# Another order of the instructions of a state-space group on four engines of a three-stage decoder layer

## The chip, the cores and the metric

The kernel runs on one core of a Trainium2 chip, as one program in one launch. The metric is the device time of that launch in microseconds (us). TensorE (PE in the profile; PEld is its weight load), VectorE (DVE), ScalarE (ACT) and GpSimd (POOL) each execute their own stream of instructions in order; SyncE (SP) issues most of the transfers. The engines are tied to each other only by semaphores: an instruction that waits holds up everything that stands behind it on its engine.

## The reference

The input x has 64 sequences of 128 tokens of 128 features. The layer is three blocks, each followed by a residual sum and a layer norm:

```
xz = x @ W_in;  xb, z = halves of xz (256 channels each)
xb = silu(causal conv of 4 taps over xb, + conv_b)
dt_low, B, C = split(xb @ W_x)           # 64, 16, 16
dt = softplus(dt_low @ W_dt + b_dt)
h[t] = h[t-1] * exp(A * dt[t]) + (x[t] * dt[t]) * B[t]   # 256 channels x 16 states
y[t] = sum over the 16 states of h[t] * C[t];  y = y + xb * D
x = layernorm(x + (y * silu(z)) @ W_out)                 # state-space block
x = layernorm(x + slots(x, context))                     # 3 rounds of slot attention and GRU
x = layernorm(x + expert(x))                             # one of 8 experts per token
```

Only the first block is touched by the change.

## The kernel before

**Stages.** `mamba_stage` (the state-space block) and `slot_stage` share one block of engine programs, `expert_stage` follows. All float32. The state-space stage treats 16 groups of 4 sequences (512 tokens), one after the other, features on the 128 partitions and tokens along the free dimension. The 256 channels are two halves c = 0, 1 and there are 16 states n, so a group has 32 units (n, c).

**One unit.** ACT computes the decays exp(A dt) of a unit (`decay`); the input (dt x) B comes in one of three ways; DVE runs the recurrence as one scan over 512 tokens (`scan`, L734); POOL multiplies both halves of the state by C (`product`, L440, written here p0 to p15) into one of four `hc` buffers; PE adds that into `ps_y` by eight transposing matmuls (`add_y`, L914).

**Three ways for the input.** States 1, 5 and 9 are fed by POOL (`feed`, L425: dtx times a row of B that a transfer has spread over the partitions). States 0, 2, 4, 8, 10, 12, 13 and 15 are fed by DVE (`feed`, L717, which reads B from the one PSUM bank `ps_b`, filled by PE in `spread_b`, L923). States 3, 6, 7, 11 and 14 are "side" states: ACT scales a transposed dtx by B (`scaled`, four instructions, L574), PE transposes it into a `ps_op` bank (`side_input`, L931), and the decays go into `da_side` instead (L564).

**Buffers that set the order.** `inp`, `state` and `hc` have four slots, used by n mod 4. A POOL feed of state n waits until scan (n-4, 1) is done, a scan (n, 0) until product n-4 is done, a product until add_y n-4 is done. The three `ps_op` banks go round over the units, so a direct decay (or the side input) of a unit waits until the scan three units earlier is done. `da_side` and `inpT` have two slots. The two `ps_misc` banks serve all the rest: the projections of the next group, the tail of the group before, and the units P, K, V0, V1, V2 that prepare the context for the slot stage.

**Across groups.** While group g is scanned, the same engines prepare group g+1 (transposed x, convolution, `silu`, `x_dbl`, B transposed, dt, dtx) and finish group g-1: DVE gates y with z after the last add_y of g-1 (`gated`, L705, in the middle of the scans of state 2), PE turns and projects it, ACT centres and squares it, and DVE multiplies by 1/std at the end of group g (`normed`, L710, whose two inputs `cent` and `lnv` both lie in SBUF). Then DVE feeds state 0 of group g+1. POOL computes dt and dtx of g+1 between products 11 and 12.

**What fixes the order.** No planner runs: in each engine's program a function `group` lists the calls by hand, and `over_groups` unrolls it 16 times (`first` and `last` leave parts out). In the text f5 is a feed of state 5, s(5,1) the scan of unit (5,1), and a prime marks the next group. SP has its own list, with waits on those engines before its transfers.

Of the kernel before, what the change touches and what calls it, by code (L numbers as in the profile page):

```python
# [12 lines left out]
P = 128  # L13
# [111 lines left out]
def mamba_stage(nc, t, sb, psum, sem, blk, tail, slot_in, x1T, ident, made, NG, NS, C, R):  # L125
# [272 lines left out]
    def _(pool):  # L398
# [43 lines left out]
        def group(g, par, first, last):  # L442
            product(g, par, first, 0)
            product(g, par, first, 1)
            product(g, par, first, 2)
            feed(g, par, 5)
            product(g, par, first, 3)
            product(g, par, first, 4)
            feed(g, par, 9)
            product(g, par, first, 5)  # L450
            product(g, par, first, 6)
            product(g, par, first, 7)
# [11 lines left out]
            product(g, par, first, 14)  # L464
            if not last:
                feed(g + 1, 1 - par, 1)
            product(g, par, first, 15)
# [3 lines left out]
    def _(act):  # L471
# [128 lines left out]
        def group(g, par, first, last):  # L600
            if not first:
                read_unit(g - 1, "V2")
            if not last:
                prepare(g + 1, 1 - par, "xT")
            decay(g, par, 1, 0)
            scaled(g, par, 3)
# [23 lines left out]
            if not first:  # L630
                turned(g - 1, 0)
# [3 lines left out]
            decay(g, par, 9, 0)  # L635
            if not last:
                prepare(g + 1, 1 - par, "BT")
            scaled(g, par, 11)
            if not last:
                prepare(g + 1, 1 - par, "relu0")  # L640
            decay(g, par, 9, 1)
            if not first:
                turned(g - 1, 1)
            if not last:
                prepare(g + 1, 1 - par, "abs0")
            decay(g, par, 10, 0)
            decay(g, par, 10, 1)
            decay(g, par, 11, 0)
            if not last:
                prepare(g + 1, 1 - par, "relu1")  # L650
                prepare(g + 1, 1 - par, "abs1")
            decay(g, par, 11, 1)
            if not last:
                prepare(g + 1, 1 - par, "exp")
            decay(g, par, 12, 0)
            decay(g, par, 12, 1)
            if not first:
                centred(g - 1)
            if not last:
                prepare(g + 1, 1 - par, "ln")  # L660
            read_unit(g, "P")
            decay(g, par, 14, 0)
            scaled(g, par, 14)
            decay(g, par, 13, 0)
            read_unit(g, "K")
            decay(g, par, 13, 1)
            decay(g, par, 14, 1)
            if not first:
                log_variance(g - 1)
                root(g - 1)  # L670
# [14 lines left out]
    def _(dve):  # L685
# [52 lines left out]
        def group(g, par, first, last):  # L738
            scan(g, par, 0, 0)
            scan(g, par, 0, 1)  # L740
            feed(g, par, 2)
            scan(g, par, 1, 0)
            scan(g, par, 1, 1)
            scan(g, par, 2, 0)
# [3 lines left out]
            scan(g, par, 3, 0)  # L748
            scan(g, par, 3, 1)
            feed(g, par, 4)  # L750
# [4 lines left out]
            feed(g, par, 8)  # L755
# [32 lines left out]
    def _(pe):  # L788
# [166 lines left out]
        def group(g, par, first, last):  # L955
            if not first:
                add_y(g - 1, 1 - par, 14)
# [3 lines left out]
            if not first:  # L961
                add_y(g - 1, 1 - par, 15)
# [1330 lines left out]
```

## Time and profile before

| | us |
|---|---|
| median of 3 runs | 1535.23 (1533.06 to 1535.28) |
| the profiled execution's own time | 1535.57 |
| its span in the profile | 1533.7 |
| busy: PE / DVE / ACT / POOL | 1375.4 / 1215.4 / 1105.4 / 1222.6 |
| mean granted clock of PE | 0.964 |

The span is what the profile covers from the first to the last instruction; the execution's own time holds 1.87 us more. Busy times are sums over the three stages. The state-space stage lasts from the start to about 850 us, the slot stage from there to some 1330 us, the expert stage to the end. In a timeline a row is one run of like instructions: start, length, engine, line, operation, output and inputs, and in brackets how long the engine sat idle before it and who released it. Neighbouring instructions of an engine overlap by some hundredths of a microsecond in such rows, so what an instruction costs on its engine is the distance between two starts.

### The profile page before, as it was taken

How to read it: one execution, taken by the hardware profiler on the slowest of the kernel's cores; microseconds unless marked ns; L12 is line 12 of the kernel's file. 1: busy time of each engine (PE TensorE's matmuls, PEld its weight loads, DVE VectorE, ACT ScalarE, POOL GpSimd, SP SyncE). 2: the span in 40 equal slices, each digit the busy share in tenths (PEclk: the TensorE clock that was granted, in tenths of full speed). 3: DMA queues.
4: the chain of work that ended last, by engine and by line, in shares of the span. 5: the costliest groups of instructions: out<-in, count | busy, mean ns of one | idle time of the engine just before them, and what ended most of it. 6: DMA issues, size and time to landing. Idle time of an engine off the chain costs nothing. (4 is left out here: it accounts for less than half of the span.)

```text
span 1533.7 us, 27686 instructions
## 1 busy us (share of the span) xinstructions
PE 1375.4 (90%) x8898; PEld 1075.9 (70%) x8898; DVE 1215.4 (79%) x2143; ACT 1105.4 (72%) x2296; POOL 1222.6 (80%) x845
## 2 busy tenths in 40 slices
PE   5999999999999999999988899999999999559993
PEld 2676766666766676677666688878888877449993
DVE  1899999999999999999999477777777777734552
ACT  3888988889888988898887666666666665115552
POOL 1899999999999999999998544577777776625665
PEclk8999999999999999999999999999999999669997
DMA  4334433434344434443341642431436000057770
GB/s 139 103 99 140 124 123 104 130 124 132 95 131 123 136 97 125 128 131 110 117 127 60 205 144 103 150 122 57 154 130 254 9 8 15 21 152 193 207 215 28
DMA packets 114560, 182.75 MB, mean 119 GB/s; under 512 B 12210, under 2 KB 75637, under 8 KB 114432
## 3 DMA queue, kind: packets, MB, share of 16 engines
q1 hardware_dynamic: 109888, 172.68, 36.5%
q0 software_dynamic: 4544, 8.47, 1.6%
q8 instruction: 67, 1.10, 0.3%
q14 instruction: 61, 0.50, 0.1%
HBM read 126.37 MB, written 55.66 MB: 119 GB/s over the span
## 5 line engine op out<-in xcount | busy, mean ns | idle before, releaser
L440 POOL TENSOR_TENSOR hc<-state,c_rows 128x1024 f32<-128x1024 f32 x256 | 599.4, 2367 | 26.4 <-DVE state L734 26.3
L734 DVE TENSOR_TENSOR_SCAN state<-ps_op,inp 128x512 f32<-128x512 f32 x352 | 406.5, 1203 | 7.8 <-issue 3.3
L914 PE MATMUL ps_y<-ident,hc 128*128 128x128 f32 x2048 | 255.5, 274 | 22.0 <-POOL hc L440 21.7
L914 PEld LDWEIGHTS ps_y<-ident,hc 128*128 128x128 f32 x2048 | 228.4, 141 | 63.9 <-POOL hc L440 47.3
L567 ACT ACTIVATE ps_op<-dt,a_neg 128x512 f32<-128x512 f32 x352 | 238.5, 690 | 40.5 <-DVE state L734 36.6
L734 DVE TENSOR_TENSOR_SCAN state<-da_side,ps_op 128x512 f32<-128x512 f32 x160 | 183.9, 1197 | 16.4 <-PE ps_op L931 16.4
L717 DVE TENSOR_TENSOR inp<-dtx,ps_b 128x1024 f32<-128x1024 f32 x128 | 153.5, 1199 | 44.1 <-POOL dtx L413 24.0
L1325 POOL TENSOR_TENSOR rs<-ms,m_half 128x4 f32<-128x4 f32 x48 | 68.0, 1416 | 117.2 <-DVE ms L1584 117.0
L1493 ACT ACTIVATE ex<-sc,nmx,ctx_r 77x128 f32<-77x128 f32 x192 | 92.4, 482 | 91.1 <-DVE nmx L1597 91.1
L574 ACT ACTIVATE inpT<-dtxT,b_tok 128x256 f32<-128x256 f32 x320 | 135.8, 499 | 0.0
L425 POOL TENSOR_TENSOR inp<-dtx,b_rows 128x1024 f32<-128x1024 f32 x48 | 120.1, 2502 | 0.0
L2103 POOL DMA_INDIRECT out_x<-orow,target x78 | 77.0, 987 | 43.4 <-ACT orow L2124 22.3
L564 ACT ACTIVATE da_side<-dt,a_neg 128x512 f32<-128x512 f32 x160 | 109.7, 715 | 0.0
L931 PEld LDWEIGHTS ps_op<-ident,inpT 128*128 128x128 f32 x640 | 73.2, 142 | 47.7 <-issue 30.5
L931 PE MATMUL ps_op<-ident,inpT 128*128 128x128 f32 x640 | 96.2, 278 | 9.3 <-DVE state L734 6.5
L923 PE MATMUL ps_b<-ident,b_tok 128*128 128x128 f32 x512 | 80.6, 281 | 25.2 <-DVE inp L717 25.2
L2134 ACT ACTIVATE act_h<-ps_h 128x512 f32<-128x512 f32 x78 | 46.5, 597 | 69.2 <-PE ps_h L2244 59.6
L923 PEld LDWEIGHTS ps_b<-ident,b_tok 128*128 128x128 f32 x512 | 58.4, 139 | 52.7 <-DVE inp L717 32.8
L1423 POOL DMA_INDIRECT sorted_x<-row,dest x60 | 62.1, 1036 | 26.4 <-issue 14.5
L2253 PEld LDWEIGHTS ps_yy<-w,act_h 128*128 128x128 f32 x624 | 75.6, 192 | 2.0
L2253 PE MATMUL ps_yy<-w,act_h 128*128 128x128 f32 x624 | 75.8, 275 | 0.0
L2244 PE MATMUL ps_h<-xcol,w 128*128 128x256 f32 x312 | 75.5, 386 | 0.0
(251 smaller groups left out, 3141.6 us busy)
## 6 DMA issues: line engine op xcount, KB each, us to landing
c_rows<-bc_rows SPq DMA_DIRECT2D x128, 512.0 KB, 3.8
sorted_x<-pad_rows SPq DMA_DIRECT2D x8, 4160.0 KB
w<-in_L_ffn_W SPq DMA_DIRECT2D x78, 256.0 KB
b_rows<-bc_rows SPq DMA_DIRECT2D x48, 256.0 KB, 4.9
vw<-vw_rows SPq DMA_DIRECT2D x16, 462.0 KB
vw_rows<-vw_out SPq DMA_DIRECT2D x16, 384.0 KB
xrow<-sorted_x SPq DMA_DIRECT2D x39, 130.0 KB
x_tok<-in_x SPq DMA_DIRECT2D x16, 256.0 KB, 4.5
```

The lines of the kernel that those rows point to most:

```text
L425: pool.tensor_tensor(inp[:, n % RING], dtx[:, par], over_c(b_rows[:, s]), ALU.mult).then_inc(pool_fed, 1)
L440: pool.tensor_tensor(hc[:, n % RING], state[:, n % RING], over_c(c_rows[:, slot, n % 2]), ALU.mult).then_inc(hc_ready, 1)
L564: act.activation(da_side[:, at % 2, c], dt[:, par, c], ACT.Exp, scale=a_neg[:, c, n:n + 1]).then_inc(side_da, 1)
L567: act.activation(op_bank(g, n, c)[:], dt[:, par, c], ACT.Exp, scale=a_neg[:, c, n:n + 1]).then_inc(da_ready, 1)
L574: ins = act.activation(inpT[:, at % 2, b], dtxT[:, b].rearrange("p c d -> p (c d)"), ACT.Copy, scale=b_tok[:, par, b, n:n + 1])
L717: dve.tensor_tensor(inp[:, n % RING], dtx[:, par], over_c(ps_b[:]), ALU.mult).then_inc(dve_fed, 1)
L734: dve.tensor_tensor_scan(state[:, n % RING, c], decays, inputs, 0.0, ALU.mult, ALU.add).then_inc(state_ready, 1)
L914: ins = pe.matmul(ps_y[:, b, c], hc[:, n % RING, c, b * P:(b + 1) * P], ident[:], start=False, stop=n == NS - 1, is_transpose=True, skip_g ...
L923: ins = pe.transpose(ps_b[:, b * P:(b + 1) * P], b_tok[:, par, b, n:n + 1].broadcast_to([P, P]), ident[:])
L931: ins = pe.transpose(op_bank(g, n, c)[:, b * P:(b + 1) * P], inpT[:, at % 2, b, c * P:(c + 1) * P], ident[:])
L1493: act.activation(ex[p][0:M, b * P:(b + 1) * P], sc[p][:, b * P:(b + 1) * P], ACT.Exp, bias=nmx[p][:, b:b + 1], scale=ctx_r[:, g % RING, b: ...
L2253: ins = pe.matmul(ps_yy[par][:, s * P:(s + 1) * P], act_h[:, par, c, s * P:(s + 1) * P], w2[:, buf, c], start=c == 0, stop=c == FC - 1)
```

## The change

Nothing is added or removed. In `group` on POOL, ACT, DVE and PE the same calls stand in another order; buffers, semaphores, the transfers of SP and the other stages are as before. On POOL, the feed of state 5 moves ahead of product 0, that of state 9 behind product 6, and that of state 1 of the next group ahead of product 14. On DVE most feeds stand one or two scans later and `normed` stays at the end. On ACT the decays of state 3 and 11 come earlier, `scaled` of 11 stands between the two loads of activation tables, and `root` comes later. On PE the side inputs and spreads are placed anew among the add_y.

```diff
--- before.py
+++ after.py
@@ pool: group @@
 def group(g, par, first, last):
+    feed(g, par, 5)
     product(g, par, first, 0)
     product(g, par, first, 1)
     product(g, par, first, 2)
-    feed(g, par, 5)
     product(g, par, first, 3)
     product(g, par, first, 4)
-    feed(g, par, 9)
     product(g, par, first, 5)
     product(g, par, first, 6)
+    feed(g, par, 9)
     product(g, par, first, 7)
     product(g, par, first, 8)
     product(g, par, first, 9)
...
     if not last:
         prepare(g + 1, 1 - par, "first")
     product(g, par, first, 13)
+    if not last:
+        feed(g + 1, 1 - par, 1)
     product(g, par, first, 14)
-    if not last:
-        feed(g + 1, 1 - par, 1)
     product(g, par, first, 15)
@@ scalar: group @@
 def group(g, par, first, last):
+    decay(g, par, 3, 0)
+    if not last:
+        prepare(g + 1, 1 - par, "xT")
+    decay(g, par, 1, 0)
+    decay(g, par, 1, 1)
     if not first:
         read_unit(g - 1, "V2")
-    if not last:
-        prepare(g + 1, 1 - par, "xT")
-    decay(g, par, 1, 0)
     scaled(g, par, 3)
-    decay(g, par, 1, 1)
     decay(g, par, 2, 0)
-    decay(g, par, 3, 0)
-    decay(g, par, 2, 1)
     decay(g, par, 3, 1)
     decay(g, par, 6, 0)
+    decay(g, par, 2, 1)
+    scaled(g, par, 6)
+    scaled(g, par, 7)
     decay(g, par, 6, 1)
-    scaled(g, par, 6)
     decay(g, par, 4, 0)
-    scaled(g, par, 7)
+    decay(g, par, 4, 1)
     decay(g, par, 7, 0)
+    decay(g, par, 5, 0)
     decay(g, par, 7, 1)
-    decay(g, par, 4, 1)
-    decay(g, par, 5, 0)
     decay(g, par, 5, 1)
     act.preload_act_table_set("silu_and_others")
     if not last:
         prepare(g + 1, 1 - par, "xb0")
         prepare(g + 1, 1 - par, "xb1")
+    scaled(g, par, 11)
     gates(g, 0)
     gates(g, 1)
     act.preload_act_table_set("natural_log_exp_and_others")
     decay(g, par, 8, 0)
+    decay(g, par, 8, 1)
+    if not last:
+        prepare(g + 1, 1 - par, "dbl")
     if not first:
         turned(g - 1, 0)
-    decay(g, par, 8, 1)
-    if not last:
-        prepare(g + 1, 1 - par, "dbl")
+    decay(g, par, 11, 0)
+    if not last:
+        prepare(g + 1, 1 - par, "BT")
     decay(g, par, 9, 0)
-    if not last:
-        prepare(g + 1, 1 - par, "BT")
-    scaled(g, par, 11)
+    decay(g, par, 9, 1)
     if not last:
         prepare(g + 1, 1 - par, "relu0")
-    decay(g, par, 9, 1)
-    if not first:
-        turned(g - 1, 1)
-    if not last:
         prepare(g + 1, 1 - par, "abs0")
     decay(g, par, 10, 0)
     decay(g, par, 10, 1)
...
+    decay(g, par, 11, 1)
+    scaled(g, par, 14)
...
-    decay(g, par, 11, 1)
+    if not first:
+        turned(g - 1, 1)
...
         prepare(g + 1, 1 - par, "exp")
     decay(g, par, 12, 0)
+    read_unit(g, "P")
+    if not last:
+        prepare(g + 1, 1 - par, "ln")
     decay(g, par, 12, 1)
+    decay(g, par, 13, 0)
     if not first:
...
+    decay(g, par, 13, 1)
     decay(g, par, 14, 0)
-    scaled(g, par, 14)
-    decay(g, par, 13, 0)
     read_unit(g, "K")
-    decay(g, par, 13, 1)
-    decay(g, par, 14, 1)
     if not first:
         log_variance(g - 1)
+    decay(g, par, 14, 1)
+    decay(g, par, 15, 0)
+    read_unit(g, "V0")
+    decay(g, par, 15, 1)
+    if not last:
+        prepare(g + 1, 1 - par, "t0")
+    if not first:
         root(g - 1)
-    read_unit(g, "V0")
-    decay(g, par, 15, 0)
-    decay(g, par, 15, 1)
+    if not last:
+        decay(g + 1, 1 - par, 0, 0)
     read_unit(g, "V1")
     if not last:
-        prepare(g + 1, 1 - par, "t0")
-        decay(g + 1, 1 - par, 0, 0)
         prepare(g + 1, 1 - par, "t1")
         decay(g + 1, 1 - par, 0, 1)
@@ vector: group @@
 def group(g, par, first, last):
     scan(g, par, 0, 0)
     scan(g, par, 0, 1)
-    feed(g, par, 2)
     scan(g, par, 1, 0)
     scan(g, par, 1, 1)
+    feed(g, par, 2)
     scan(g, par, 2, 0)
     if not first:
         gated(g - 1)
     scan(g, par, 2, 1)
     scan(g, par, 3, 0)
+    feed(g, par, 4)
     scan(g, par, 3, 1)
-    feed(g, par, 4)
     scan(g, par, 4, 0)
...
     scan(g, par, 5, 1)
-    feed(g, par, 8)
...
-    feed(g, par, 10)
+    feed(g, par, 8)
     scan(g, par, 8, 0)
     scan(g, par, 8, 1)
+    feed(g, par, 10)
...
     scan(g, par, 11, 0)
+    feed(g, par, 12)
     scan(g, par, 11, 1)
-    feed(g, par, 12)
     feed(g, par, 13)
     scan(g, par, 12, 0)
     scan(g, par, 12, 1)
+    scan(g, par, 13, 0)
     feed(g, par, 15)
-    scan(g, par, 13, 0)
     scan(g, par, 13, 1)
     scan(g, par, 14, 0)
     scan(g, par, 14, 1)
@@ tensor: group @@
 def group(g, par, first, last):
+    spread_b(g, par, 2)
+    if not last:
+        fill_misc(g + 1, 1 - par, "xb1")
     if not first:
         add_y(g - 1, 1 - par, 14)
-    spread_b(g, par, 2)
-    if not last:
-        fill_misc(g + 1, 1 - par, "xb1")
+    if not last:
+        fill_misc(g + 1, 1 - par, "xb0")
     if not first:
         add_y(g - 1, 1 - par, 15)
-    if not last:
-        fill_misc(g + 1, 1 - par, "xb0")
+    side_input(g, 3, 0)
+    side_input(g, 3, 1)
     spread_b(g, par, 4)
-    side_input(g, 3, 0)
     if not last:
         fill_misc(g + 1, 1 - par, "xb0+")
-    side_input(g, 3, 1)
+        fill_misc(g + 1, 1 - par, "xb1+")
     start_y(g, par)
-    if not last:
-        fill_misc(g + 1, 1 - par, "xb1+")
     add_y(g, par, 0)
     add_y(g, par, 1)
-    add_y(g, par, 2)
     spread_b(g, par, 8)
     side_input(g, 6, 0)
+    add_y(g, par, 2)
     side_input(g, 6, 1)
     fill_z(g, 0, last)
+    side_input(g, 7, 0)
     fill_z(g, 1, last)
-    side_input(g, 7, 0)
-    spread_b(g, par, 10)
     side_input(g, 7, 1)
...
     add_y(g, par, 3)
+    spread_b(g, par, 10)
     if not last:
         fill_misc(g + 1, 1 - par, "BT")
-    add_y(g, par, 4)
     if not first:
         turn_y(g - 1, 1)
+    if not last:
+        fill_misc(g + 1, 1 - par, "dt0")
+    add_y(g, par, 4)
+    if not last:
+        fill_misc(g + 1, 1 - par, "dt1")
+    side_input(g, 11, 0)
     add_y(g, par, 5)
+    spread_b(g, par, 12)
     add_y(g, par, 6)
+    side_input(g, 11, 1)
     add_y(g, par, 7)
-    if not last:
-        fill_misc(g + 1, 1 - par, "dt1")
     add_y(g, par, 8)
-    side_input(g, 11, 0)
-    side_input(g, 11, 1)
+    fill_unit(g, "P", last)
+    spread_b(g, par, 13)
     if not first:
         project(g - 1)
-    fill_unit(g, "P", last)
+    spread_b(g, par, 15)
     add_y(g, par, 9)
-    spread_b(g, par, 13)
-    spread_b(g, par, 15)
+    add_y(g, par, 10)
     fill_unit(g, "K", last)
     if not first:
...
     side_input(g, 14, 0)
-    add_y(g, par, 10)
+    side_input(g, 14, 1)
     fill_unit(g, "V0", last)
-    side_input(g, 14, 1)
+    if not last:
+        fill_misc(g + 1, 1 - par, "t0")
     add_y(g, par, 11)
     if not last:
         spread_b(g + 1, 1 - par, 0)
     fill_unit(g, "V1", last)
     if not last:
-        fill_misc(g + 1, 1 - par, "t0")
+        fill_misc(g + 1, 1 - par, "t1")
     add_y(g, par, 12)
-    fill_unit(g, "V2", last)
-    if not last:
-        fill_misc(g + 1, 1 - par, "t1")
+    add_y(g, par, 13)
     if g + 2 < NG:
         fill_misc(g + 2, par, "xT")
-    add_y(g, par, 13)
+    fill_unit(g, "V2", last)
```

## Rows read from the trace of the kernel before

**Rows 1.** The page: busy time, share of the span and instructions, by engine.
```profile
PE 1375.4 (90%) x8898; PEld 1075.9 (70%) x8898; DVE 1215.4 (79%) x2143; ACT 1105.4 (72%) x2296; POOL 1222.6 (80%) x845
```
**Rows 2.** Busy time in one period of group 7 (stretch, length, engines, PE clock, DMA).
```profile
391.81:442.40 50.59, 46.94 (x294) 34.16 (x293) 48.08 (x43) 45.09 (x81) 49.35 (x24) 1.00 0.41 121
```
**Rows 3.** Timeline of POOL over one period (start, length, what, idle before).
```profile
391.81 2.83 POOL L425 TENSOR_TENSOR inp<-dtx,b_rows 128x1024 f32<-128x1024 f32 x1
394.61 4.67 POOL L440 TENSOR_TENSOR hc<-state,c_rows 128x1024 f32<-128x1024 f32 x2
399.45 2.38 POOL L440 TENSOR_TENSOR hc<-state,c_rows 128x1024 f32<-128x1024 f32 x1 [0.18 <-DVE state L734]
402.81 2.36 POOL L440 TENSOR_TENSOR hc<-state,c_rows 128x1024 f32<-128x1024 f32 x1 [0.98 <-DVE state L734]
405.12 2.38 POOL L425 TENSOR_TENSOR inp<-dtx,b_rows 128x1024 f32<-128x1024 f32 x1
...
414.41 16.29 POOL L440 TENSOR_TENSOR hc<-state,c_rows 128x1024 f32<-128x1024 f32 x7
430.66 2.35 POOL L409 TENSOR_TENSOR dt<-relu,softp 128x1024 f32<-128x1024 f32 x1
...
435.41 2.38 POOL L440 TENSOR_TENSOR hc<-state,c_rows 128x1024 f32<-128x1024 f32 x1
...
442.40 2.84 POOL L425 TENSOR_TENSOR inp<-dtx,b_rows 128x1024 f32<-128x1024 f32 x1
```
**Rows 4.** Timeline of DVE over the same period.
```profile
390.53 1.88 DVE L710 TENSOR_TENSOR x1T<-cent,sq 128x512 f32<-128x512 f32 x1
392.34 1.21 DVE L717 TENSOR_TENSOR inp<-dtx,ps_b 128x1024 f32<-128x1024 f32 x1
393.68 2.34 DVE L734 TENSOR_TENSOR_SCAN state<-ps_op,inp 128x512 f32<-128x512 f32 x2
...
411.79 4.54 DVE L734 TENSOR_TENSOR_SCAN state<-da_side,ps_op 128x512 f32<-128x512 f32 x4
...
425.45 2.33 DVE L734 TENSOR_TENSOR_SCAN state<-da_side,ps_op 128x512 f32<-128x512 f32 x2 [0.95 <-PE ps_op L931]
...
429.95 1.22 DVE L717 TENSOR_TENSOR inp<-dtx,ps_b 128x1024 f32<-128x1024 f32 x1 [1.05 <-PE ps_b L923]
```
**Rows 5.** Timeline of POOL in the first and in the last group.
```profile
40.25 2.35 POOL L440 TENSOR_TENSOR hc<-state,c_rows 128x1024 f32<-128x1024 f32 x1 [1.14 <-DVE state L734]
46.43 4.69 POOL L440 TENSOR_TENSOR hc<-state,c_rows 128x1024 f32<-128x1024 f32 x2 [3.83 <-DVE state L734]
...
807.79 2.36 POOL L440 TENSOR_TENSOR hc<-state,c_rows 128x1024 f32<-128x1024 f32 x1 [1.00 <-DVE state L734]
...
838.47 2.38 POOL L440 TENSOR_TENSOR hc<-state,c_rows 128x1024 f32<-128x1024 f32 x1 [2.81 <-DVE state L734]
841.83 7.42 POOL L440 TENSOR_TENSOR hc<-state,c_rows 128x1024 f32<-128x1024 f32 x3 [0.98 <-DVE state L734]
```
**Rows 6.** Timeline of DVE at the end of the last group.
```profile
846.12 0.93 DVE L710 TENSOR_TENSOR x1T<-cent,sq 128x512 f32<-128x512 f32 x1
```
**Rows 7.** Timeline of ACT: first group, then `scaled` and the table load of group 7.
```profile
42.20 0.70 ACT L567 ACTIVATE ps_op<-dt,a_neg 128x512 f32<-128x512 f32 x1
...
393.07 1.70 ACT L574 ACTIVATE inpT<-dtxT,b_tok 128x256 f32<-128x256 f32 x4
...
408.17 1.28 ACT L622 ACT_TABLE_LOAD   x1
...
412.85 1.28 ACT L628 ACT_TABLE_LOAD   x1
414.15 0.69 ACT L567 ACTIVATE ps_op<-dt,a_neg 128x512 f32<-128x512 f32 x1
```
**Rows 8.** Timeline of PE in group 7: add_y of product 15, and half a convolution.
```profile
397.01 1.09 PE L914 MATMUL ps_y<-ident,hc 128*128 128x128 f32 x8 [1.05 <-POOL hc L440]
397.94 1.88 PE L806 MATMUL ps_misc<-x1T,w_conv 128*128 128x512 f32 x4
```

More of the change, by code:

```diff
@@ L463, in group @@
             product(g, par, first, 13)
-            product(g, par, first, 14)
             if not last:
                 feed(g + 1, 1 - par, 1)
+            product(g, par, first, 14)
             product(g, par, first, 15)
@@ L605, in group @@
             decay(g, par, 1, 0)
+            decay(g, par, 1, 1)
+            if not first:
+                read_unit(g - 1, "V2")
             scaled(g, par, 3)
-            decay(g, par, 1, 1)
             decay(g, par, 2, 0)
-            decay(g, par, 3, 0)
-            decay(g, par, 2, 1)
             decay(g, par, 3, 1)
             decay(g, par, 6, 0)
+            decay(g, par, 2, 1)
+            scaled(g, par, 6)
+            scaled(g, par, 7)
             decay(g, par, 6, 1)
-            scaled(g, par, 6)
             decay(g, par, 4, 0)
-            scaled(g, par, 7)
+            decay(g, par, 4, 1)
             decay(g, par, 7, 0)
+            decay(g, par, 5, 0)
             decay(g, par, 7, 1)
-            decay(g, par, 4, 1)
-            decay(g, par, 5, 0)
             decay(g, par, 5, 1)
@@ L629, in group @@
             decay(g, par, 8, 0)
-            if not first:
-                turned(g - 1, 0)
             decay(g, par, 8, 1)
@@ L634, in group @@
                 prepare(g + 1, 1 - par, "dbl")
-            decay(g, par, 9, 0)
+            if not first:
+                turned(g - 1, 0)
+            decay(g, par, 11, 0)
             if not last:
                 prepare(g + 1, 1 - par, "BT")
-            scaled(g, par, 11)
+            decay(g, par, 9, 0)
+            decay(g, par, 9, 1)
             if not last:
                 prepare(g + 1, 1 - par, "relu0")
-            decay(g, par, 9, 1)
+                prepare(g + 1, 1 - par, "abs0")
+            decay(g, par, 10, 0)
+            decay(g, par, 10, 1)
+            if not last:
+                prepare(g + 1, 1 - par, "relu1")
+            decay(g, par, 11, 1)
+            scaled(g, par, 14)
+            if not last:
+                prepare(g + 1, 1 - par, "abs1")
             if not first:
@@ L955, in group @@
         def group(g, par, first, last):
-            if not first:
-                add_y(g - 1, 1 - par, 14)
             spread_b(g, par, 2)
@@ L961, in group @@
             if not first:
-                add_y(g - 1, 1 - par, 15)
+                add_y(g - 1, 1 - par, 14)
             if not last:
                 fill_misc(g + 1, 1 - par, "xb0")
+            if not first:
+                add_y(g - 1, 1 - par, 15)
+            side_input(g, 3, 0)
+            side_input(g, 3, 1)
             spread_b(g, par, 4)
-            side_input(g, 3, 0)
             if not last:
                 fill_misc(g + 1, 1 - par, "xb0+")
-            side_input(g, 3, 1)
+                fill_misc(g + 1, 1 - par, "xb1+")
             start_y(g, par)
-            if not last:
-                fill_misc(g + 1, 1 - par, "xb1+")
             add_y(g, par, 0)
             add_y(g, par, 1)
-            add_y(g, par, 2)
             spread_b(g, par, 8)
             side_input(g, 6, 0)
+            add_y(g, par, 2)
             side_input(g, 6, 1)
             fill_z(g, 0, last)
+            side_input(g, 7, 0)
             fill_z(g, 1, last)
-            side_input(g, 7, 0)
-            spread_b(g, par, 10)
             side_input(g, 7, 1)
@@ L988, in group @@
             add_y(g, par, 3)
+            spread_b(g, par, 10)
             if not last:
                 fill_misc(g + 1, 1 - par, "BT")
+            if not first:
+                turn_y(g - 1, 1)
+            if not last:
+                fill_misc(g + 1, 1 - par, "dt0")
             add_y(g, par, 4)
             if not last:
-                fill_misc(g + 1, 1 - par, "dt0")
+                fill_misc(g + 1, 1 - par, "dt1")
+            side_input(g, 11, 0)
+            add_y(g, par, 5)
             spread_b(g, par, 12)
-            if not first:
-                turn_y(g - 1, 1)
-            add_y(g, par, 5)
             add_y(g, par, 6)
+            side_input(g, 11, 1)
             add_y(g, par, 7)
-            if not last:
-                fill_misc(g + 1, 1 - par, "dt1")
             add_y(g, par, 8)
-            side_input(g, 11, 0)
-            side_input(g, 11, 1)
+            fill_unit(g, "P", last)
+            spread_b(g, par, 13)
             if not first:
                 project(g - 1)
-            fill_unit(g, "P", last)
+            spread_b(g, par, 15)
             add_y(g, par, 9)
-            spread_b(g, par, 13)
-            spread_b(g, par, 15)
+            add_y(g, par, 10)
             fill_unit(g, "K", last)
```

10 lines of the change are left out of this document (1 added, 9 removed).

## The prediction

> **What bounds the kernel now.** I read the busy line first [rows 1]: PE is busiest by name, but its rows overlap, and over the whole span nothing is full. The share has to be read in the stage that the change touches. The stretch table for one period of group 7 [rows 2] has POOL busy 49.35 of 50.59 us, DVE 48.08, PE 46.94 and ACT 45.09. The reader should see two engines within 5% of the period, and POOL the fuller one.
>
> The timeline of POOL says the same from start to start [rows 3]. The feed of state 1 starts at 391.81 and again at 442.40, so the period is 50.59 us. POOL is idle in it twice: 0.18 us ahead of p1 (399.45) and 0.98 us ahead of p2 (402.81), both released by a scan. The rest, 50.59 - 1.16 = 49.43 us, is work; I use 49.4. Its price list: a product 2.32 us (seven take 16.25 us, 414.41 to 430.66), f5 as a feed without a neighbour 2.3, dt and dtx together 4.75 (430.66 to 435.41), the feed of state 1 2.79 (391.81 to 394.61, two hundredths off by rounding).
>
> The price of that last feed, and the two idle times, have one cause, which the timeline of DVE shows [rows 4]. `normed` starts at 390.53 and takes 1.88 us. In the last group the same instruction takes 0.93 us [rows 6], so its length isn't work. In both places it ends about 0.6 us after POOL's next instruction could begin: 390.53 + 1.88 = 392.41 = 391.81 + 0.60 in group 7. In the last group the three products from 841.83 cost 7.42 us [rows 5] where three at 2.32 are 7.0. So `normed` waits for the POOL instruction in flight to end, then runs 0.6 us, and POOL's next one loses 0.47 us (2.79 against 2.32). The Trainium skill says so of the pair of SBUF ports that the two engines share (SBUF — State Buffer, Who interferes with whom): a DVE instruction with two SBUF inputs and a GpSimd one that reads SBUF exclude each other, for a whole instruction. By that rule, and the rows agree, the time of `normed` moves in steps of one POOL instruction.
>
> Now the cycle that makes 50.59 closes. From the end of p14 (391.81) DVE needs normed 0.53, the feed of state 0 1.34 (392.34 to 393.68), then s(0,0) to s(2,1) with one feed and `gated` between, eight steps of 1.12 us, to release p2 at 402.81, 11.0 us later. From p2 POOL runs without a gap to the end of the next p14. DVE's own waits for PE, 0.95 and 1.05 us [rows 4], lie ahead of the port wait and are swallowed by it.
>
> **The change, part by part.** Nothing is added to any list, so every term is a wait.
>
> POOL, feed of state 5 moved ahead of p0: it needs scan (1,1) only. Where POOL came to p2 after two products and needed s(2,1), it now comes to f5 straight behind p15 and needs s(1,1), and reaches p2 one instruction later; the close meeting moves from s(2,1) to s(1,1). With t = 0 at the start of f5 and POOL never idle: p0 2.3, p1 4.7, p2 7.0, p3 9.3, p5 13.9, f9 18.6, p8 23.2, p11 30.2, dt 32.5, dtx 34.9, p12 37.2, p13 39.6, feed 1' 41.9, p14 44.7, p15 47.0, next f5 49.4. If `normed` is queued before p13 ends at 41.9, it goes there; then the feed of state 0' is at 42.4, s(0,0)' at 43.8, and s(1,1)' ends at 48.35, or t = -1.0 of the next group. f5 finds it ready with 1.0 us to spare. No row shows POOL waiting for s(1,1) at f5, so I bound that wait by 0 and by the 0.98 us of p2 before; I take 0, and keep the upper end for the rival called leaks. Below nothing it can't go, since POOL's own work stays.
>
> DVE from there, with steps of 1.12 us (three steps and 1.19 are the 4.54 of four scans [rows 4]) and 1.34 where a scan reads the feed just ahead of it: s(2,1) ends at 3.8 (p2 wants it at 7.0), s(3,1) 7.2 (p3 9.3), s(5,1) 11.7 (p5 13.9), s(8,1) 19.7 (p8 23.2), s(11,1) 29.0 (p11 30.2, the narrowest), s(15,1) 40.4. In it are three waits that I find by laying the new lists of ACT and PE beside each other: `gated` 0.15 us, since half a convolution (steps of 1.7 us, from the 1.88 of [rows 8]) now stands ahead of add_y 15 (1.09, same rows); s(9,0) 0.4 us for f9, which starts later and ends at 20.9; the feed of state 13 0.3 us for its spread. They replace the two of 0.95 and 1.05. So `normed` is queued at 40.4, 1.5 us before the 41.9 at which it must be there. That 1.5 us is the cover of every wait not seen.
>
> ACT: 45.09 us of work in 49.4 [rows 2]. Its dangerous stretch is table load, two silu, `scaled` of 11, two gates, table load, decay (8,0). `scaled` (1.6 us of pitch, 1.70 in [rows 7]) is new in it. I get the first table load at 9.1, `scaled` at 11.95 (it waits for side input (6,1)), decay (8,0) done at 16.7, and s(8,0) wants it at 17.4: hidden by 0.7 us, and costing DVE one for one beyond that. A load costs 1.30 us from start to the next start (412.85 to 414.15 [rows 7]). The Trainium skill (ScalarE: Activation LUTs, What ACT_TABLE_LOAD costs) gives 1283 ns and 1380 ns of drain behind it, about 2.66 us in all. The trace doesn't show the drain here; by the page's figure decay (8,0) would be 2.8 us later, DVE would miss 41.9, and the rival of one step below would hold. I go by the rows.
>
> PE: 46.94 us in 49.4, 2.5 us of slack [rows 2]. The closest meetings I find are side input (14,0), ready 0.2 us before s(14,0), and side (7,1), 0.4 us before s(7,1). If each such meeting came 0.5 us late instead, the 1.5 us would just be spent. The transfers of C rows follow products p1, p3, ... as before, and the first user is six products behind; moved feeds release the B rows more than 15 us before use. `root` is done at 39.2, before `normed`. I cost all these at nothing; without that cover the price is that of a POOL step.
>
> **Sum.** (a) First group: p0 ran at 40.25 in the shade of the start-up, p1 from 46.43, p2 from 46.43 + 2.31 = 48.74 [rows 5]. Now f5 stands first and waits for s(1,1). Decay (1,0) started at 42.20 after the copy of x [rows 7] and still does, so the scan goes at 42.9, s(1,1) ends at 45.2, f5 starts at 45.3 and p2 at 52.3: +3.5 us. (b) From p2 of group 0 to p2 of group 15: before 807.79 - 48.74 = 759.05 us; now 14 periods of 49.4 and one without `normed` of 48.9, 740.5 us: -18.5. (c) Last group, p2 to the end of p15: p15 ended at 841.83 + 7.42 = 849.25, so before 849.25 - 807.79 = 41.46, with 2.81 and 0.98 of waits [rows 5]. Now POOL is held by DVE from p12 on; s(15,1) ends at 40.4, p15 runs from 40.5 to 43.3 with the 0.47 of the port, and 43.3 - 7.0 = 36.3: -5.1. Together -20.1 us, of which 2.3 in (a) and (c) is f5 changing sides of p2. The stages behind shift as they are. That assumes a POOL without a gap of even a tenth in 15 periods; I give back 0.07 us in each, 1 us. The profiled execution has 1535.57 us (its span of 1533.7 and 1.87 around it), so 1535.57 - 19.1 = 1516.5; the median before is 0.34 lower, which gives 1516.
>
> **Rivals.** *One step late.* If DVE's waits in a group reach some 1.5 us more than I found, `normed` misses the end of p13 and goes at the end of the feed of state 1', at 44.2. Then s(1,1)' ends at 44.2 + 0.53 + 1.34 + 4.56 + a hand-off of 0.1 = 50.75, and that is the period. (b) becomes 14 x 50.75 + 48.9 = 759.4, (a) + (b) + (c) = 3.5 + 0.4 - 5.1 = -1.2 us: 1534, no change. For it: the old waits of 2.00 us, kept in full and added to the 0.85 that I count, would do it. Against: both belonged to places in the PE list that have moved (spread 13 stood behind three adds and `project`, side input 11 behind add_y 8).
>
> *Two steps late,* the slower side. The same port: should DVE be held 3.4 us or more (the point is `normed` queued after 44.2 in the slower cycle), it goes at the end of p14, 2.32 us later again. The period is 53.1, (b) grows by 14 x 2.32 = 32.5: 1566. The place would be the ACT block around the table loads. For it: `scaled` 11 in the block, 0.7 us of cover. Against: the block would have to be 4 us longer than ACT's rows make it.
>
> *Leaks.* `normed` makes its step, but POOL meets late scans, at p11 or at f5 itself, for 0.3 to 1.0 us a group: 15 times that on 1515, so 1520 to 1530. For it: POOL has only 1.0 us in hand at f5 and 1.2 at p11. Against: DVE's schedule has 1.5 us of rest before the port in every group.
>
> *The order does nothing,* since another engine bounds the period. DVE has 48.08 us with 1.3 of port wait in it and the others less, so none reaches 50.6; I count it with one step late.
>
> **How the numbers follow.** Forecast 0.70 (1513 to 1519), leaks 0.14, one step late 0.10, two steps 0.06. A measurement can tell about 0.2%, 3 us, from no change. Faster by more is the forecast and the leaks: 0.84. Within 0.2%: 0.10. Slower: 0.06. The range 1512 to 1531 holds forecast and leaks with their bounds, 0.84 less the tails, and leaves the two late cases out. Below 1512 POOL would need less than its own work.
>
> **What would show it.** Right: a period of 49.4 from one feed of state 1 to the next; no idle of POOL within a group; the feed still 2.8; `normed` ending 0.6 us behind the end of p13, with a length between 1.5 and 2.5 us; DVE idle below 1.5 us a group, mainly at s(9,0) and the feed of state 13. Wrong: `normed` ending behind the feed of state 1' or p14; POOL waiting for scan (1,1) at f5 in every group (then the port cycle still rules); ACT's decay (8,0) released later than s(7,1); a PE clock below 1.00 in the middle groups, where two gaps on PE grow together.

## The result, and the profile after

The changed kernel takes 1517.93 us (median of 4 runs, 1516.06 to 1518.79) against 1535.26 of the kernel before, a ratio of 0.9891 with a 95% interval of 0.9879 to 0.9903: 17.3 us faster. The forecast was 1516. The profiled execution has a span of 1516.3 us.

The busy line of the page, and below it the stretch table for one period in mid-run (stretch, length, PE, PEld, DVE, ACT, POOL, PE clock, DMA share, GB/s), which answers to [rows 2]:

```profile
PE 1366.7 (90%) x8898; PEld 1080.4 (71%) x8898; DVE 1218.3 (80%) x2143; ACT 1099.4 (73%) x2296; POOL 1220.9 (81%) x845
```
```profile
386.03:435.41 49.38, 46.35 (x292) 34.39 (x292) 48.36 (x43) 44.78 (x81) 49.30 (x23) 1.00 0.40 125
```

The work is the same, and POOL fills 49.30 of 49.38 us. Its timeline over that period, beside [rows 3], has no bracket with an idle time left:

```profile
386.03 2.83 POOL L425 TENSOR_TENSOR inp<-dtx,b_rows 128x1024 f32<-128x1024 f32 x1
388.82 4.68 POOL L440 TENSOR_TENSOR hc<-state,c_rows 128x1024 f32<-128x1024 f32 x2
393.46 2.37 POOL L425 TENSOR_TENSOR inp<-dtx,b_rows 128x1024 f32<-128x1024 f32 x1
395.79 16.30 POOL L440 TENSOR_TENSOR hc<-state,c_rows 128x1024 f32<-128x1024 f32 x7
...
433.10 2.37 POOL L440 TENSOR_TENSOR hc<-state,c_rows 128x1024 f32<-128x1024 f32 x1
435.41 2.82 POOL L425 TENSOR_TENSOR inp<-dtx,b_rows 128x1024 f32<-128x1024 f32 x1
```

And DVE's, beside [rows 4]:

```profile
387.89 4.57 DVE L737 TENSOR_TENSOR_SCAN state<-ps_op,inp 128x512 f32<-128x512 f32 x4
...
414.55 4.57 DVE L737 TENSOR_TENSOR_SCAN state<-ps_op,inp 128x512 f32<-128x512 f32 x4 [0.30 <-POOL inp L425]
...
422.77 1.22 DVE L720 TENSOR_TENSOR inp<-dtx,ps_b 128x1024 f32<-128x1024 f32 x1 [0.31 <-PE ps_b L926]
...
433.97 2.04 DVE L713 TENSOR_TENSOR x1T<-cent,sq 128x512 f32<-128x512 f32 x1
435.94 1.21 DVE L720 TENSOR_TENSOR inp<-dtx,ps_b 128x1024 f32<-128x1024 f32 x1
```

`normed` (L713 now) is queued at 433.97 and p13 ends at 435.41, so it lies 1.44 us ahead of its step; it ends at 436.01, 0.60 us behind it. The four scans from 387.89 end at 392.46, and f5 starts at 393.46, 1.0 us later. The two waits of 0.95 and 1.05 us for PE are gone, and 0.30 and 0.31 stand in their place.

Two things in the trace weren't forecast. POOL waits for an add_y in group 5, in group 13 and in the last one. The first of them on POOL, then PE ahead of it, then PE's stretch table:

```profile
320.22 7.02 POOL L440 TENSOR_TENSOR hc<-state,c_rows 128x1024 f32<-128x1024 f32 x3 [0.80 <-PE ps_y L917]
```
```profile
315.35 1.12 PE L832 MATMUL ps_misc<-xdbl,w_dt 64*128 64x512 f32 x2 [0.33 <-ACT softp L506]
317.41 0.97 PE L934 MATMUL ps_op<-ident,inpT 128*128 128x128 f32 x4 [0.94 <-DVE state L737]
318.17 1.91 PE L917 MATMUL ps_y<-ident,hc 128*128 128x128 f32 x8
```
```profile
316.00:320.00 4.00, 3.06 (x15) 2.62 (x14) 4.00 (x5) 3.82 (x8) 3.43 (x2) 0.69 0.41 142
```

The eight matmuls of an add_y take 1.91 us here and 1.09 in [rows 8]. The granted clock averages 0.69 over these 4 us, so part of them ran at the lower of its two levels (1.2 GHz, not 2.4), behind idle times of 0.33 and 0.94 us on PE. The same two gaps stand in every group from 1 to 14; in twelve of these fourteen the clock stays at 1.00.

The time of the whole splits as follows. "Stage" is from POOL's first dt to the end of the last product. It leaves out the start-up, which ended anywhere between 31.7 and 34.8 us in the traces of this study, whatever the kernel.

| | median us | ratio to before, 95% | period us | stage us |
|---|---|---|---|---|
| before | 1535.26 | | 50.61 | 817.5 |
| changed | 1517.93 | 0.9891 [0.9879, 0.9903] | 49.38 | 800.6 |
| after_again | 1519.50 | 0.9903 [0.9887, 0.9920] | 49.38 | 800.2 |
| stretch2 | 1531.85 | 0.9978 [0.9963, 0.9993] | 49.38, then 50.85 | 810.0 |
| stretch4 | 1540.89 | 1.0040 [1.0028, 1.0053] | 50.85 | 823.0 |
| stretch6 | 1592.88 | 1.0380 [1.0363, 1.0397] | 54.61 | 875.1 |
| after_one_sbuf | 1513.85 | 0.9858 [0.9841, 0.9876] | 48.9 to 49.7 | 795.5 |
| before_one_sbuf | 1521.14 | 0.9913 [0.9896, 0.9930] | 49.57 | 802.7 |
| pool_only | 1572.51 | 1.0228 [1.0211, 1.0245] | 52.35 | 851.1 |
| all_but_pool | 1528.47 | 0.9943 [0.9926, 0.9960] | 49.74 | 806.3 |
| rest_feed1 | 1517.59 | 0.9885 [0.9869, 0.9902] | 49.38 | 799.2 |
| add5_first | 1517.83 | 0.9872 [0.9856, 0.9888] | 49.37 | 798.4 |
| rest_add5 | 1522.41 | 0.9911 [0.9891, 0.9931] | 49.72 | 802.5 |
| both | 1516.53 | 0.9875 [0.9857, 0.9892] | 49.38 | 796.2 |

The first two rows belong together. The others come from three chips: the `stretch` rows and after_one_sbuf from one, pool_only, all_but_pool, add5_first and rest_add5 from a second, the rest from a third. On these the kernel before took 1534.98, 1536.91 and 1535.23 us, so a row is read by its ratio to the kernel before on the same chip. Period and stage are those of one profiled execution each.

### The profile page after: what moved, and what is told of

It is laid out like the page before. It is cut to its first block and busy times, and to the rows that moved or that the text cites. A ratio compares the mean times of both kernels' runs of the same rounds, so it can differ in the third digit from the quotient of the medians.

```text
span 1516.3 us, 27686 instructions
## 1 busy us (share of the span) xinstructions
PE 1366.7 (90%) x8898; PEld 1080.4 (71%) x8898; DVE 1218.3 (80%) x2143; ACT 1099.4 (73%) x2296; POOL 1220.9 (81%) x845
## 5 line engine op out<-in xcount | busy, mean ns | idle before, releaser
L917 PE MATMUL ps_y<-ident,hc 128*128 128x128 f32 x2048 | 264.1, 276 | 23.2 <-POOL hc L440 23.1
L917 PEld LDWEIGHTS ps_y<-ident,hc 128*128 128x128 f32 x2048 | 232.6, 143 | 67.4 <-POOL hc L440 44.6
L934 PE MATMUL ps_op<-ident,inpT 128*128 128x128 f32 x640 | 93.0, 277 | 19.4 <-DVE state L737 19.3
L934 PEld LDWEIGHTS ps_op<-ident,inpT 128*128 128x128 f32 x640 | 75.8, 143 | 43.8 <-issue 40.4
```

The lines of the kernel that those rows point to most:

```text
L917: ins = pe.matmul(ps_y[:, b, c], hc[:, n % RING, c, b * P:(b + 1) * P], ident[:], start=False, stop=n == NS - 1, is_transpose=True, skip_g ...
L934: ins = pe.transpose(op_bank(g, n, c)[:, b * P:(b + 1) * P], inpT[:, at % 2, b, c * P:(c + 1) * P], ident[:])
```

## The experiments

In the expectations, "port theory" is the prediction's account: `normed` waits for the POOL instruction in flight, runs between it and the next, and so moves in steps of one POOL instruction.

### Does `normed` move in steps of a POOL instruction?

Three runs hold `normed` back, by two, four and six DVE reductions of 0.6 us each ahead of the last scan of a group. The edit with two, its declaration of `spare` left out:

```diff
         def scan(g, par, n, c):
...
+            if (n, c) == (15, 1):
+                for k in range(2):
+                    dve.tensor_reduce(spare[:, k:k + 1], decays, AX_X, ALU.add)
             dve.tensor_tensor_scan(state[:, n % RING, c], decays, inputs, 0.0, ALU.mult, ALU.add).then_inc(state_ready, 1)
```

> Changed kernel with four extra DVE reductions (2.4 us) ahead of the last scan of each group. Port theory: `normed` misses the end of p13 and goes behind the feed of state 1'; the period jumps to 50.75, 14 x 1.37 = 19 us plus 2.4 in the last group: 1537 to 1540, with POOL idle 1.3 us at f5. Rival (DVE's sum decides): 46.7 + 2.4 + 0.6 = 49.7 us, 14 x 0.3 + 2.4 = 7 us more: 1524 to 1526.

Measured: 1540.89 us, 0.9 above the range, and a period of 50.85, where the prediction's second cycle had 50.75. DVE and POOL of that run:

```profile
443.03 1.93 DVE L714 TENSOR_TENSOR x1T<-cent,sq 128x512 f32<-128x512 f32 x1
```
```profile
442.05 2.35 POOL L426 TENSOR_TENSOR inp<-dtx,b_rows 128x1024 f32<-128x1024 f32 x1
444.37 5.12 POOL L441 TENSOR_TENSOR hc<-state,c_rows 128x1024 f32<-128x1024 f32 x2
450.93 2.37 POOL L426 TENSOR_TENSOR inp<-dtx,b_rows 128x1024 f32<-128x1024 f32 x1 [1.44 <-DVE state L741]
```

`normed` is queued 1.0 us behind the start of the feed of state 1' (1.3 in most groups), so it waits to 444.37, ends 0.6 us later, and the loss of 0.46 us has moved from the feed (2.35 now) to the products behind it (5.12 for two). POOL idles 1.44 us at f5. The rival by sums is out: it had 1524 to 1526.

> Changed kernel with two extra DVE reductions (about 0.6 us each, results unused) ahead of the last scan of each group, so `normed` is queued 1.2 us later. Port theory: it is still queued before p13 ends (1.44 us of rest in the changed trace), so the period stays 49.4; only the last group, whose end hangs on DVE, is 1.2 us longer: 1518 to 1520. Rival (DVE's sum of work decides, no steps): DVE's 46.7 us of work and 0.6 of waits become 48.5, still under POOL's 49.4: the same 1518 to 1520.

Measured: 1531.85 us. Both theories missed. The period is 49.38 seven times (behind a first one of 48.9, without `normed`), once 50.1, and then 50.85 to the end. Where it turns:

```profile
515.72 7.03 POOL L441 TENSOR_TENSOR hc<-state,c_rows 128x1024 f32<-128x1024 f32 x3 [0.74 <-PE ps_y L921]
...
541.03 2.37 POOL L426 TENSOR_TENSOR inp<-dtx,b_rows 128x1024 f32<-128x1024 f32 x1 [1.43 <-DVE state L741]
```

With 1.2 us of reductions the queueing point lies 0.2 to 0.3 us ahead of the step. Ahead of the row at 515.72 PE's clock falls (0.72 on average from 512 to 518). POOL loses 0.74 us by it and DVE, which waits 1.16 us for a spread there, some 1.7, so `normed` is queued at 532.78, 0.6 us behind the end of p13, and the kernel never comes back: six groups in a row wait 1.43 to 1.45 us at f5. In the slower cycle f5 starts just behind its scan, not 1.0 us behind, so DVE starts each group that much later against POOL; this reason for its lasting is read from the trace, not tested. Two cycles last in the same kernel, and 1.2 us of extra work cost some 13 us by the ratios (0.9978 against 0.9891). The seven runs spread from 1526.74 to 1535.01 us, which would fit a slip in another group each time; only the one trace shows where.

> Changed kernel with six extra DVE reductions (3.6 us) ahead of the last scan of each group. Port theory: second step, `normed` behind p14, period 53.1, 14 x 3.7 = 52 us plus 3.6: 1571 to 1575. Rival (DVE's sum decides): 50.9 us, 14 x 1.5 + 3.6 = 25 us more: 1541 to 1544.

Measured: 1592.88 us, above either. Period 54.61, with 3.76 us of idle at f5, so the second step is taken; 1.5 us a group more than 53.1 remain, of which 1.16 us is p9 waiting for add_y 5, in nearly every group. PE's clock has a part in it, though not at the gap ahead of that add_y. With `normed` late, the feed of state 0' is late, and PE idles 3.99 us for it. The clock falls there in every period from 197 us on (0.53 on average from 416 to 423) and is back at 1.00 before 423, long before p9 waits:

```profile
417.26 1.12 PE L930 MATMUL ps_b<-ident,b_tok 128*128 128x128 f32 x4 [3.99 <-DVE inp L721]
418.17 3.61 PE L813 MATMUL ps_misc<-x1T,w_conv 128*128 128x512 f32 x4
```
```profile
425.73 1.23 DVE L709 TENSOR_TENSOR yz<-ps_y,sz 128x1024 f32<-128x1024 f32 x1 [1.35 <-PE ps_y L921]
```
```profile
449.05 7.02 POOL L441 TENSOR_TENSOR hc<-state,c_rows 128x1024 f32<-128x1024 f32 x3 [1.15 <-PE ps_y L921]
```

Half a convolution takes 3.61 us where [rows 8] has 1.88, the add_y behind it is late, `gated` waits 1.35 us, and from there DVE is late against POOL for side input (11,0), add_y 5 and p9. The last links are read from the rows; how much of the 1.16 us comes from the clock and how much from the later start of DVE isn't separated.

### Is it a conflict over the inputs in SBUF?

```diff
         def normed(g):
             dve.wait_ge(act_tail, atail("rstd", g))
-            dve.tensor_tensor(x_slot(g), cent[:], lnv[:], ALU.mult).then_inc(x1_ready, 1)
+            if g == NG - 1:
+                dve.tensor_tensor(x_slot(g), cent[:], lnv[:], ALU.mult).then_inc(x1_ready, 1)
+                return
+            if g + 2 < NG:
+                dve.wait_ge(b_spread, fed_count(DVE_FEEDS, g + 2, 0))
+            dve.tensor_tensor(x_slot(g), cent[:], ps_b[:], ALU.mult).then_inc(x1_ready, 1)
```

> Changed kernel in which `normed` takes its second input from the PSUM bank ps_b instead of the SBUF tile, in the groups 0 to 14 (so x1 is wrong, the normalisation is left out; same size, same count). Port theory: no wait for POOL and no loss on POOL's next feed: `normed` 0.6 us, the feed of state 1 2.32 instead of 2.79, period 48.9, 14 x 0.47 = 6.6 us less: 1510 to 1512. Rival (the 2.04 us of `normed` and the 2.8 us of the feed have other causes, as reading a tile just written): both lengths stay and so does the time, 1517 to 1519.

Measured: 1513.85 us. `normed` takes 0.66 us, all of the feeds of state 1 take 2.35 to 2.42, and the period is 48.9 to 49.0 in nine of its groups:

```profile
432.00 0.66 DVE L718 TENSOR_TENSOR x1T<-cent,ps_b 128x512 f32<-128x512 f32 x1
```
```profile
433.43 2.37 POOL L425 TENSOR_TENSOR inp<-dtx,b_rows 128x1024 f32<-128x1024 f32 x1
```

The instruction has another second operand, in another memory, and one semaphore wait more, for which DVE doesn't idle here; both the wait for POOL and POOL's loss of 0.47 us are gone. The trace of the changed kernel has the opposite case too: the `normed` of the last group, with both inputs in SBUF, runs while POOL is idle, and takes 0.68 us:

```profile
853.10 0.68 DVE L713 TENSOR_TENSOR x1T<-cent,sq 128x512 f32<-128x512 f32 x1
```

So two SBUF inputs alone don't make it long, nor does a tile just written; it is the two inputs meeting a POOL instruction, as the prediction had it. The time is 2 us above the forecast's upper end. In the groups 1 to 14 products waited five times for an add_y, 2.7 us in all, where the changed kernel has two such waits, 1.5 us together; that is 1.2 of it.

> The kernel before in which `normed` takes its second input from the PSUM bank ps_b instead of the SBUF tile, in the groups 0 to 14 (the normalisation is left out; same size, same count). Port theory: `normed` 0.6 us instead of 1.88 and the feed of state 1 2.35, so the chain from p14 to p2 is cut and POOL's 48.95 us or DVE's 49.3 decide: 14 x 1.3 to 1.6 us less, 1513 to 1518. Rival (DVE's waits for PE set POOL's idle time by themselves): they grow by what `normed` gives, and the time stays at 1530 to 1536.

Measured: 1521.14 us, 3.1 above the range: 14.1 us below the kernel before, where 17 to 22 were expected. The period of 49.57 keeps 0.6 us of idle at p2:

```profile
436.41 0.66 DVE L715 TENSOR_TENSOR x1T<-cent,ps_b 128x512 f32<-128x512 f32 x1
```
```profile
437.58 2.37 POOL L425 TENSOR_TENSOR inp<-dtx,b_rows 128x1024 f32<-128x1024 f32 x1
439.89 7.01 POOL L440 TENSOR_TENSOR hc<-state,c_rows 128x1024 f32<-128x1024 f32 x3
447.47 2.37 POOL L440 TENSOR_TENSOR hc<-state,c_rows 128x1024 f32<-128x1024 f32 x1 [0.56 <-DVE state L739]
```

One operand, with all old lists in place, gives most of what the reordering gave (14.1 us, against 15.7 for `after_again` on the same chip). So the port wait carried the old period. Of the 0.6 us that stays at p2, DVE's own waits (0.87 and 1.05 us for PE there, and about 0.5 ahead of s(10,0)) are the likely cause; no run takes them away with `normed` cut short.

### Which list does it?

`pool_only` is the kernel before with POOL's `group` of the changed one, `all_but_pool` the changed kernel with POOL's old one.

> The kernel before with only POOL's list in the new order. Port theory: f5 now waits for scan (1,1), which DVE's old list reaches one feed later; with `normed` at the end of p13 the period is 41.9 + 7.6 = 49.55, and with it one step later 51.9. DVE's queueing point falls 0.3 to 0.9 us before the end of p13, with all its old waits for PE, so it is one of two values: 1519 to 1522 where it is reached in every group, up to 1553 where it is missed, and one between where a slip in mid-run isn't made good. Rival (POOL's new order by itself removes POOL's idle time): 1516 to 1518.

Measured: 1572.51 us, 36 us slower than before; both theories missed. DVE, then POOL:

```profile
436.88 4.66 DVE L734 TENSOR_TENSOR_SCAN state<-ps_op,inp 128x512 f32<-128x512 f32 x4 [1.07 <-POOL inp L425]
443.11 2.33 DVE L734 TENSOR_TENSOR_SCAN state<-da_side,ps_op 128x512 f32<-128x512 f32 x2 [1.57 <-PE ps_op L931]
...
458.80 1.86 DVE L710 TENSOR_TENSOR x1T<-cent,sq 128x512 f32<-128x512 f32 x1
```
```profile
460.05 5.14 POOL L440 TENSOR_TENSOR hc<-state,c_rows 128x1024 f32<-128x1024 f32 x2
468.11 2.37 POOL L425 TENSOR_TENSOR inp<-dtx,b_rows 128x1024 f32<-128x1024 f32 x1 [2.92 <-DVE state L734]
```

f9 comes later in POOL's new list and now makes s(9,0) wait 1.07 us, which pushes the old wait for PE from 0.95 to 1.57; `normed` is queued behind the start of the feed of state 1' (it waits to 460.05), and f5, behind the old position of DVE's feed of state 2, waits 2.92 us. It is the late cycle, with the period 52.35 where I had 51.9. The forecast's upper value is still 20 us short. The stage is 33.6 us longer than before: 25.9 lie in the 14 periods, which run from 52.1 to 53.0, and 7.7 in the first and last group, for which the expectation had no price.

> The changed kernel with POOL's old list; DVE, ACT and PE in the new order. Port theory: DVE's waits for PE shrink from 2.0 to some 0.5 us, so `normed` is queued 1.9 us before the end of p13 and goes one POOL instruction earlier than before; p2 then finds its scan ready (0.8 us of rest) and the period is POOL's own 49.4. The first group keeps p0 ahead of f5, 1 to 2 us better than the changed kernel: 1515 to 1518. Rival (the moves on POOL are needed, since POOL's two idle times lie in front of p1 and p2): they stay, 1532 to 1536.

Measured: 1528.47 us, 8 us faster than before, neither of the two. The new lists of the three others do move `normed` one step earlier, but the period is 49.74:

```profile
443.46 2.34 DVE L737 TENSOR_TENSOR_SCAN state<-ps_op,inp 128x512 f32<-128x512 f32 x2 [1.08 <-POOL inp L425]
```
```profile
440.97 2.36 POOL L425 TENSOR_TENSOR inp<-dtx,b_rows 128x1024 f32<-128x1024 f32 x1
...
450.59 2.36 POOL L440 TENSOR_TENSOR hc<-state,c_rows 128x1024 f32<-128x1024 f32 x1 [0.30 <-DVE state L737]
```

With `normed` earlier, s(1,0)' arrives before its own feed, which stands behind p14 in POOL's old list, and waits 1.08 us; p2 pays 0.30. I had overlooked that feed. One move should mend it (the lists of the two runs against each other):

```diff
             product(g, par, first, 13)
+            if not last:
+                feed(g + 1, 1 - par, 1)
             product(g, par, first, 14)
-            if not last:
-                feed(g + 1, 1 - par, 1)
             product(g, par, first, 15)
```

> DVE, ACT and PE new, POOL's old list with one move, the feed of state 1' ahead of p14. Theory: the 1.08 us that scan (1,0) waits for this feed and the 0.30 us of p2 behind it go, the period is 49.4 instead of 49.74: 1520 to 1524. Rival (f5 ahead of p0 is what frees p2): still 0.3 us at p2, 1527 to 1529.

Measured: 1517.59 us, 2.4 below the range and 9 below the rival's, period 49.38, no wait of POOL in the groups 1 to 14. That equals the changed kernel (0.9885 against 0.9903 for `after_again` beside it, the intervals overlap). The moves of f5 and f9, which the prediction put first, aren't needed. Which of the three other lists, on DVE, ACT and PE, is needed was not tried.

### PE's clock, and the first group

```diff
-            side_input(g, 11, 0)
             add_y(g, par, 5)
+            side_input(g, 11, 0)
             spread_b(g, par, 12)
```

> The changed kernel with one pair on PE swapped: add_y 5 ahead of side input (11,0), which fills the gap of 0.95 us in which PE waits for a scan. Theory: in two groups and in the last one PE's granted clock fell behind that gap and a product waited 0.80, 0.68 and 1.20 us for add_y; these go: 1514 to 1517, and no POOL row with a wait for ps_y in the groups 1 to 14. Rival (the drops come by chance and anywhere): two or three such rows stay, 1517 to 1519.

Measured: 1517.83 us, above the forecast's range and inside the rival's, though on a chip on which the kernel before took 1.7 us more. But no product of any group waits for an add_y, and the stage is 798.4 us against 800.2 to 800.6. The gap is filled:

```profile
415.25 1.09 PE L917 MATMUL ps_y<-ident,hc 128*128 128x128 f32 x8
416.26 0.63 PE L934 MATMUL ps_op<-ident,inpT 128*128 128x128 f32 x4
```

The ratio of 0.9872 overlaps that of the changed kernel (0.9891); a gain of 2 us is seen in the stage of one trace but not proven in the total.

For the gap as the place of the drops the traces say more together than this one. Where it is 0.88 to 0.97 us (46 groups in the traces of the changed kernel, taken twice, of stretch2 up to its slip and of after_one_sbuf), the clock fell at it in 9. Where it is 0.75 us or less (52 groups, among them all of rest_feed1 with 0.73 and of all_but_pool and stretch4 with 0.51), or filled (42 groups of add5_first, rest_add5 and both), it fell at this place in none. The length of a single gap isn't the rule, though: in the groups 2 to 14, idle times of 1.31 us in the kernel before and of 1.69 in stretch4 passed at 1.00. What decides in which groups the clock falls isn't shown.

> POOL's old list, the other three new, and the same swap on PE. Port theory: both gains add: 1512 to 1516. Rival: as for the two runs by themselves, 1532 to 1536.

Measured: 1522.41 us, between the two ranges; the stage is 3.8 us shorter than in `all_but_pool`, where add_y had made POOL wait 2.65 us in the first and the last group, and here not at all. The totals don't separate (the intervals of the ratios meet). The level was expected too low because the period stays at 49.72: the 0.35 us that the feed of state 1' costs in each group was missing from the expectation.

> The changed kernel again, on the chip of the next two, as the thing to compare them with: 1516 to 1519, two or three products a run waiting 0.7 to 1.2 us for add_y behind a drop of PE's granted clock.

Measured: 1519.50 us (1515.99 to 1520.57), 0.5 above the range. The profiled run has two such waits: 0.81 us in group 9, where the first trace had them in groups 5 and 13, and 1.19 us in the last group, as there (1.20).

> The changed kernel with add_y 5 ahead of side input (11,0) on PE, and in the first group alone p0 ahead of f5 on POOL. Theory: p0 fits into the 6.3 us that POOL idles for scan (1,1), so 2.3 us less, and the clock drops are gone, 2 us less: 4 us below the changed kernel on the same chip, 1512 to 1515. Rival (the start of the first group is hidden by something else, as the first products' C rows or add_y): 2 us below at most.

Measured: 1516.53 us, 1.5 above the range; 3.0 below the changed kernel on the same chip, and 4 in the stage. p0 runs at 42.44 in the gap ahead of f5:

```profile
42.44 2.36 POOL L440 TENSOR_TENSOR hc<-state,c_rows 128x1024 f32<-128x1024 f32 x1 [1.14 <-DVE state L740]
47.59 2.37 POOL L425 TENSOR_TENSOR inp<-dtx,b_rows 128x1024 f32<-128x1024 f32 x1 [2.80 <-DVE state L740]
```

By the median it is faster than both kernels; its interval [0.9857, 0.9892] just meets that of `after_again` [0.9887, 0.9920], so the gain over the changed kernel is likely, not shown.

## Why the prediction was right, point by point

**What bounds.** POOL's work of 49.4 us a group: the period after is 49.38. The port wait of `normed` as the link that closed the old cycle: shown by `before_one_sbuf`, and that it takes two SBUF inputs by both `one_sbuf` runs. Its step of one POOL instruction: shown by `stretch4`. The text said at its start that the engines are tied to each other only by semaphores; this wait, which no semaphore asks for, is a second tie.

**DVE's schedule.** Waits of 0.15, 0.4 and 0.3 us were forecast at `gated`, s(9,0) and the feed of state 13; measured 0.12 (1.24 us from 393.70 to 394.94), 0.30 and 0.31. The rest ahead of the port: 1.5 forecast, 1.44 measured. The hand in front of f5: 1.0 and 1.0.

**ACT.** Decay (8,0) was to be done 0.7 us before s(8,0). It starts at 409.42 and s(8,0) at 410.80, so with 0.69 us of length 0.7 is left. The table load costs 1.30 us from start to start (408.12 to 409.42); the drain that the Trainium skill gives (ScalarE: Activation LUTs, What ACT_TABLE_LOAD costs) isn't seen, and its rival didn't come.

**The sum.** (a) First dt to p2: 17.0 us before, 54.48 - 33.83 = 20.65 after, +3.6 for +3.5. (b) p2 to p2 over 15 groups: 759.05 before, 796.06 - 54.48 = 741.6 after, -17.5 for -18.5. The missing 1.1 us is the two waits for add_y, 0.80 and 0.68 us, less 0.3 for a period of 49.38 and not 49.4; it is just about the 1 us that I had given back for leaks. (c) Last group, p2 to the end: 834.43 - 796.06 = 38.4 after, -3.1 for -5.1. This term was mis-sized by 2 us. The last group has no work on PE for a next one, so PE idles more (2.61 and 1.23 us at its start, 3.96 ahead of side input (11,0)), and its clock falls at both places. As forecast, POOL is held by DVE from p12 on, so the 1.20 us that p9 waits for add_y 5 aren't what the end hangs on; DVE's waits are: 0.60 us at `gated`, 1.16 at the feed of state 13 and 0.40 between, together 2.2 where the forecast had 0.85 (the 0.4 at s(9,0) didn't come). s(15,1) ends 42.3 us after the start of f5 and not 40.4:

```profile
812.89 1.09 PE L934 MATMUL ps_op<-ident,inpT 128*128 128x128 f32 x4 [3.96 <-DVE state L737]
813.77 1.91 PE L917 MATMUL ps_y<-ident,hc 128*128 128x128 f32 x8
```
```profile
791.20 1.23 DVE L708 TENSOR_TENSOR yz<-ps_y,sz 128x1024 f32<-128x1024 f32 x1 [0.60 <-PE ps_y L917]
...
820.09 1.22 DVE L720 TENSOR_TENSOR inp<-dtx,ps_b 128x1024 f32<-128x1024 f32 x1 [1.16 <-PE ps_b L926]
```

Together -16.9 in the stage against -20.1 (-19.1 with the leaks). The start-up took 2.1 us more in this trace and the later stages 2.6 us less, and that these nearly cancel is luck. The change touches neither: over all traces the start-up ends between 31.7 and 34.8 us (33.8 and 32.1 in the two of the changed kernel), and the later stages take 681.9 to 686.0.

One sign of being wrong came in part: a PE clock below 1.00 in the middle groups, in two of fourteen. The cause named for it, two gaps on PE close together, fits the rows; it cost 1.5 us and not the forecast.

**What was right only in sum.** The text put the move of f5 first, as what shifts the close meeting from s(2,1) to s(1,1). It does, but `rest_feed1` shows that the gain doesn't need it. Two things make it: the new lists of DVE, ACT and PE, whose shorter waits of DVE bring `normed` to the end of p13 (`all_but_pool`), and the feed of state 1' ahead of p14, which the text listed and gave no price (`rest_feed1`). Which of the three lists shortens the waits is not separated. And "cover of 1.5 us for every wait not seen" was too kind: `stretch2` shows that with 1.2 of it used, one drop of the clock tips the kernel into the slower cycle for the rest of the stage.

## What to carry to other kernels

When two engines are both within 5% of the period, look for a short instruction of each cycle that waits for the other engine's instruction in flight: here its place relative to that engine's boundaries set the period, in steps. An order by hand is one object over all lists: POOL's new list alone cost 36 us, the other three alone gave 8, together 17 (all but one of the moves on POOL could stay out). Price every feed that a faster neighbour will now reach first, and keep rest ahead of such a step, since a miss can last.

## What the runs showed of the hardware

A DVE product of 512 columns with both inputs in SBUF waits for the POOL instruction in flight, then takes 0.6 us and costs POOL's next one 0.46 to 0.47; with one input in PSUM it takes 0.66 us at any time and costs POOL nothing, and with two in SBUF and POOL idle 0.68. The Trainium skill (SBUF — State Buffer, Who interferes with whom) has the rule, and the traces agree. DVE got its turn between two POOL instructions that stand back to back, in every group.

PE's granted clock fell in single groups behind idle times of 0.33 and 0.94 us on PE, although the same gaps passed in most groups without it, and in the last group, where PE idled 3.96 us. With the second gap filled by work that was ready it didn't fall there in 42 groups of three traces; nor did it with 0.73 or 0.51 us of gap.
